# Moving four of a batch tile's gathers from layer 1 of the tile before it to layer 2 of the tile before that, with GpSimd's products moved the other way

## The reference

```python
e = jnp.stack([tbl_0[ids[:, 0]], ..., tbl_31[ids[:, 31]]], axis=1)       # (1024, 32, 16)
xk = x0 = e
for W in (W0, W1, W2):                                                   # (32, Hk-1, 64)
    xk = relu(einsum('bmd,bhd,mhk->bkd', x0, xk, W))
    outs.append(sum(xk, axis=2))
h = concatenate([concatenate(outs, axis=1), dense_ctx], axis=1)          # 192 + 16 columns
h = maximum(h @ W_top1 + b_top1, 0); h = maximum(h @ W_top2 + b_top2, 0)
y = h @ W_top3
```

## Time and profile before

| | us |
|---|---|
| median of three runs | 651.5 |
| the profiled execution | 648.11 |
| its span | 646.1 |
| PE, DVE, POOL, ACT busy in the span | 576.5, 558.0, 513.1, 349.6 |
| one round in the middle (322.9 to 393.8) | 70.9 |
| DVE, PE, POOL busy in that round | 70.38, 69.69, 61.67 |

### The profile page before, as it was taken

One profiled execution on the slowest core, in us unless ns is written; L12 is line 12 of the kernel. 1 busy time (PEld: TensorE's weight loads), 2 busy tenths in 40 slices (PEclk: granted clock), 3 DMA queues, 4 the chain that ended last, 5 costly groups with the idle time before them and its releaser, 6 DMA issues.

```text
span 646.1 us, 8375 instructions
## 1 busy us (share of the span) xinstructions
PE 576.5 (89%) x2992; PEld 194.5 (30%) x2992; DVE 558.0 (86%) x520; ACT 349.6 (54%) x537; POOL 513.1 (79%) x373
## 2 busy tenths in 40 slices
PE   0027799999999699999999999999999999999998
PEld 0002112322343133432243223432343324333444
DVE  1002899899998699999999999999999999999993
ACT  0002664455665357666666557555667657656751
POOL 6777769488888888888888888888898876477770
PEclk9999899999999899999999999999999999999999
DMA  8649998990189925996399918995499829890000
GB/s 258 175 46 249 244 203 203 245 228 4 11 173 228 240 63 98 230 214 167 33 224 196 237 26 165 224 189 130 71 252 204 182 27 219 166 280 5 1 2 0
DMA packets 89386, 98.70 MB, mean 153 GB/s; under 512 B 60833, under 2 KB 67362, under 8 KB 89330
## 3 DMA queue, kind: packets, MB, share of 16 engines
q1 hardware_dynamic: 77058, 90.12, 63.6%
q0 software_dynamic: 8192, 2.11, 3.3%
q10 hardware_dynamic: 4096, 5.95, 2.9%
HBM read 95.00 MB, written 7.61 MB: 159 GB/s over the span
## 4 chain that ended last, share of the span: by engine, by line
DVE 39%; PE 17%; issue 10%; ACT 6%; DMA 5%; SPq 0%; DVEq 0%
DVE z L760 37%; PE acc L529 15%; DMA x0rep<-x_rows 5%; ACT xk L615 4%; DVE row_sums L742 2%; ACT xk L590 1%; ACT xk L608 1%; PE top L446 1%; ACT xk_copy L626 0%; PE top L437 0%; PE top L434 0%; SPq L307 0%; PE acc L525 0%; PE acc L486 0%; DVEq L758 0%
## 5 line engine op out<-in xcount | busy, mean ns | idle before, releaser
L760 DVE TENSOR_TENSOR z<-xk,x0rep 128x1024 f32<-128x1024 f32 x463 | 530.3, 1228 | 42.2 <-DMA x0rep<-x_rows 27.5
L529 PE MATMUL acc<-z,w_sb 128*64 128x512 f32 x1852 | 443.8, 601 | 22.7 <-DVE z L760 20.4
L412 POOL TENSOR_TENSOR z_pool<-x0rep,xk_copy 128x1024 f32<-128x1024 f32 x113 | 268.3, 2377 | 48.3 <-PE acc L529 30.7
L366 POOL DMA_INDIRECT emb<-tbl,idx x256 | 244.7, 956 | 68.7 <-issue 61.7
L529 PEld LDWEIGHTS acc<-z,w_sb 128*64 128x64 f32 x1852 | 123.1, 137 | 309.3 <-issue 158.6
L615 ACT ACTIVATE xk<-xk_copy 32x1024 f32<-32x1024 f32 x128 | 130.5, 1019 | 111.4 <-DVE z L760 110.2
L529 PE MATMUL acc<-z_pool,w_sb 128*64 128x512 f32 x452 | 116.3, 593 | 0.4 <-POOL z_pool L412 0.4
L626 ACT ACTIVATE xk_copy<-acc 64x512 f32<-64x512 f32 x128 | 75.2, 587 | 2.2 <-PE acc L529 1.0
L608 ACT ACTIVATE xk<-lay 128x1024 f32<-128x1024 f32 x16 | 16.4, 1028 | 85.2 <-DVE z L760 48.3
L423 PE MATMUL acc<-w_sb 128*64 128x512 f32 x48 | 12.8, 678 | 44.0 <-DMA emb<-tbl,idx 44.0
L529 PEld LDWEIGHTS acc<-z_pool,w_sb 128*64 128x64 f32 x452 | 31.8, 137 | 62.5 <-issue 58.1
(11 more groups left out here) (40 smaller groups left out, 91.0 us busy)
## 6 DMA issues: line engine op xcount, KB each, us to landing
x0rep<-x_rows SPq DMA_DIRECT2D x128, 512.0 KB, 16.5
lay<-x_rows SPq DMA_DIRECT2D x32, 512.0 KB, 10.8
emb<-tbl,idx POOLq DMA_INDIRECT x256, 2.7
w_long<-w ACTq DMA_DIRECT2D x4, 768.0 KB, 6.8
squares<-x_rows SPq DMA_DIRECT2D x16, 128.0 KB, 2.2
x_rows<-emb SPq DMA_DIRECT2D x7, 256.0 KB, 4.6
x_rows<-emb SPq DMA_DIRECT2D x9, 128.0 KB, 6.1
w_sb<-w_long ACTq DMA_DIRECT2D x8, 128.0 KB
```

What stands on the lines that cost most here:

```text
L366: pool.indirect_dma_start(out=emb[:, i % 2, m, :], out_offset=None, in_=tables[m], in_offset=bass.IndirectOffsetOnAxis(ap=idx[:, i, m:m + ...
L412: pool.tensor_mul(z_pool[:, (count - 1) % POOL_RING, :], x0rep[:, g % X0_GROUPS, slot, :], xk_copy[:, side, :]).then_inc(z_pool_ready, 1)
L529: mm = pe.matmul(bank[c * H:(c + 1) * H, :], w[:, tile, :], src[:, c * COLS:(c + 1) * COLS], start=(k == 0), stop=last)
L760: dve.tensor_mul(z[:, (count - 1) % RING, :], xk[:, bank, :], src).then_inc(z_ready, 1)
```

## The change

The number of gathers in layer 2 goes from 16 to 20 of a tile's 32, and those in layer 1 from 16 to 12. POOL's share of products goes from 3 to 4 in 1A and 1B of tiles 1 to 6, and from 4 to 2 in 2B of tiles 1 to 5. In tile 0, 2B goes from 4 to 3. The shares of tile 7, and those of layer 2 in tile 6, stay at 5. In a full round POOL keeps 13 products and 32 gathers, and DVE 59 products. Over the kernel DVE makes 462 products where it made 463.

```diff
     if i == 0:
-        return {(1, A): 0, (1, Bs): 5, (2, A): 3, (2, Bs): 4}[layer, side]
+        return {(1, A): 0, (1, Bs): 5, (2, A): 3, (2, Bs): 3}[layer, side]
     if i == NT - 1 or (i == NT - 2 and layer == 2):
         return 5
-    return 4 if (layer, side) == (2, Bs) else 3
+    return {(1, A): 4, (1, Bs): 4, (2, A): 3, (2, Bs): 2}[layer, side]
...
-POOL_AT = {0: (), 3: (4, 8, 11), 4: (3, 6, 9, 11), 5: (2, 4, 6, 8, 10)}
+POOL_AT = {0: (), 2: (5, 10), 3: (4, 8, 11), 4: (3, 6, 9, 11), 5: (2, 4, 6, 8, 10)}
...
-EARLY = 16
+EARLY = 20
```

## The result

The changed kernel takes 646.31 us in the median of 11 runs (644.28 to 648.74). The kernel before took 650.75 us on the same chip in 11 runs (648.97 to 655.32). The ratio, taken over all runs and not from the two medians (which lie 4.4 us apart), is 0.9916, with a 95% interval of 0.9893 to 0.9938: 5.5 us faster, between 4.0 and 7.0. The forecast was 2.3 us faster, 649.2 us. The sign was right and the time lies in the range, 0.3 us from its lower end, but about half of the gain was not in the sum (2.1 of 4.4 us by the medians, 3.2 of 5.5 by the ratio).

What follows compares the result with a forecast made beforehand. It took DVE's 70.4 us round and a 70.9 us loop through A's load as bounds, PE at the end. Of PE's 4.1 us lead 2.3 would arrive: 651.5 - 2.3 = 649.2 us, range 646.0 to 653.0.

Steps and rivals of the forecast that it cites:

- the first step: Tile 2's last gather: four more gathers hide in POOL's idle time before 2B of tile 0; load and release 2.7 us sooner.
- A's path around the loop: Later rounds, release to release through POOL's 1B, last gather and A's load: 29.3 + 41.7 = 71.0 us.
- the loop as bound: Middle rounds of the kernel before: a path closing through A's load sets 70.92 us, above DVE's own 70.4.
- what is given back in tile 7: Tile 7's landing moves only 1.9 us sooner, so of PE's 4.1 us ahead 2.3 reach the end.
- the 0.4 us in hand: 1B of tile 7: DVE's product is ready 0.4 us before PE takes it, added to the gain reaching the end.
- The straight line: Release behind A's issue, interpolated on how far B follows A: 40.7 us at 15.2, 42.7 at 22.6; slope 0.27.
- the whole lead arrives: Rival: spare transfer time in tile 7 or rounds of 70.4 us let 4.1 us or more reach the end; 647.3 us, 22%.
- A longer loop: Rival: A's load takes 42.7 us whatever B does and gathers add 0.25; rounds of 72.25 us, 654.9 us in all, 11%.
- PE's clock: Rival: the granted clock falls in the longer 2B of the steady rounds, costing 5 us; 654.2 us, 3%.
- wait for `z_pool`: Sign of a wrong forecast: PE waits in 2B for POOL's products; they were expected about 60 us after release, wanted at 64.
- the DVE wait of 1 to 2.5 us: Sign of a right forecast: in 0B of tile 7 DVE waits for `x0rep`, or ACT's second fill, 1 to 2.5 us.
- faster by over 0.5%: Whole kernel: outcome class beyond measurement noise, from most of the 647.3 us rival and the forecast's top; 28%.

Runs made afterwards that it cites:

- before_front: Kernel before with all eight gathers of 1B dealt out ahead of POOL's first product of 1B; ratio 1.0019.
- before_again: Kernel before, unchanged, run again for a second trace; 692.27 us on the slow-starting kind of chip.
- before_third: Kernel before, unchanged, run for a third trace; 687.05 us on the slow-starting kind of chip.
- after_again: Changed kernel, unaltered, run again for a second trace; ratio 0.9964 to the kernel before on the chip of 690 us.
- after_third: Changed kernel, unaltered, run once more beside its two parts; ratio 0.995 to the kernel before on a chip of 688 to 690 us.
- y_late_before: Kernel before with the wait for y, the ctx transfer and y's write moved behind side B's load; ratio 0.9909.
- y_late_after: Changed kernel with the wait for y, the ctx transfer and y's write moved behind side B's load; 641.17 us, ratio 0.9838 to the kernel before.
- run 40: Not a follow-up run: part of the sentence that on some chips the first 100 us take 40 us longer.

## Why the prediction was right or wrong

**Right: the first step.** The load of tile 2 starts 2.78 us sooner (2.7 forecast). POOL's product at 126.71 still has 5.15 us idle before it, so the four gathers were hidden:

```profile
126.71 2.37 POOL L412 TENSOR_TENSOR z_pool<-x0rep,xk_copy 128x1024 f32<-128x1024 f32 x1 [5.15 <-issue]
...
171.14 0.98 POOL L366 DMA_INDIRECT emb<-tbl,idx  x1 [0.16 <-issue]
```

Of it 1.75 reached the release in this trace, not 2.7: A's load took 41.8 us against 40.7, with B following by the same 15.2. The mean of three traces each is 2.6.

**Right: A's path around the loop.** Tile 3's POOL in 1B, first product and the tile's last gather:

```profile
301.39 2.38 POOL L412 TENSOR_TENSOR z_pool<-x0rep,xk_copy 128x1024 f32<-128x1024 f32 x1 [0.52 <-issue]
...
312.27 0.98 POOL L366 DMA_INDIRECT emb<-tbl,idx  x1 [0.16 <-issue]
```

Release to first product 9.42 us (9.44 forecast), to the end of the gather 11.86 (11.85), to A's issue 8.28 (8.00), to the release of tile 4 41.76 (41.7): 71.3, with the only wait of the middle in it, 0.96 us. B is issued 48.8 us behind the release (49.5).

**Wrong in its reason, small in effect: the loop as bound.** The prediction read 9.44 + 10.79 + 8.00 + 42.69 = 70.92 as a loop that closes through A. Any start splits a round into terms that sum to it; that they do is no sign of a bound. before_front took 1.6 to 6.2 us out of the first three terms in tiles 4 to 7 and the fourth, 42.69, grew to 44.5, 47.7, 48.6 and 50.6. The bound was B: 50.87 + 20.05. With it, the change is good for the round: B's path is 2 us shorter (48.8 + 20.05 = 68.9), A's is longer by one product less one gather (29.6 + 41 = 70.6 with a load as in tiles 3, 5 and 6), and what is left is DVE's 70.3 in three rounds of four. I had 71.0 for all. The four rounds took 282.3 us where I had 283.4, and this 1.0 us made good the 0.95 that was missing at tile 2's release. That the table agrees at tile 6 (2.38 for 2.15) is luck in this pair of traces.

**The step that failed: what is given back in tile 7.** "The landing moves by 1.1 + 0.27 x 3.0 = 1.9 us." It moved by 3.28. Here B follows A by 23.0 us before, 20.1 after, and the release comes 41.2 and 39.2 behind A's issue, 18.2 and 19.1 behind B's. The slope on B's start is 2.1 in 3.0, 0.7, not 0.27: B's load was the bound in this tile of before too. The other traces have it as well: the release is 42.2 and 41.1 us behind A's issue in before_again and before_third, 39.4 and 39.8 in after_again and after_third. ACT's second fill of 0B in after:

```profile
569.68 1.03 ACT L608 ACTIVATE xk<-lay 128x1024 f32<-128x1024 f32 x1 [5.57 <-DMA lay<-x_rows]
```

It ends at 570.71, before at 573.79, 3.1 sooner. With 3.28 for 1.9, and the 0.4 us in hand as forecast, the sum gives 3.7 us, and the traces show 3.53. The straight line was drawn through 15.2 and 22.6 as if they lay on one slope; they lay on two sides of a bend. The prediction's rival "the whole lead arrives" (22%) comes near in its number, 4.2 us, but its reason, spare time in tile 7, does not hold: in before slot 2 of B landed at 574.49, 0.1 us ahead of the product that needs it, and in after DVE waits 1.22 us for it. The lead came through because the landing moved with B's issue.

**Not in the sum at all: what the timed runs have beyond the traces.** The step above is worth 1.4 us of the 3.2 that the sum lacks. The first two traces differ by 3.53 us behind the start and 3.2 in all, the timed runs by 5.5 (4.0 to 7.0). The profiled execution of before (648.11) is below all 11 timed ones beside it, though one run of the same kernel on the other chip of this kind took 646.37; that of after (644.91) lies among its own. Late landings like the one in tile 3 of before_again cost the kernel before whatever they last. B has 1.4 us of spare in after (70.3 - 68.9), so small ones should cost it less. That is argued, not shown: the changed kernel's three traces lie 4.5 us apart, those of before 5.4, and the dip behind y's write is in both kernels. Some 2 us of the gain stay open.

**Rivals.** A longer loop did not come: rounds stayed at 70.3 to 71.3. PE's clock stayed at 1.00 in the middle. PE did not wait for `z_pool`. Tile 7 shows the DVE wait of 1 to 2.5 us that was told, 1.22.

**The chance.** I gave "faster by over 0.5%" 28%. The arithmetic moved the median in step with the trace, 648.11, though the times on hand put the median 3.4 us above it. A trace that beats all timed runs was a reason to look for what the slower ones suffer from, and to widen on the fast side.

## What to carry to other kernels

A release that waits for two loads in one queue is the later of two sums, not a weighted mean: work out both paths, and find where the second load's issue falls after the first has drained. A chain of terms that adds up to the round proves nothing; what shows that a path is not the bound is that one of its terms grows when another is shortened. And look at what stands in the queue ahead of a large load: a few bytes per partition at that place can cost as much as a whole rearrangement gains.

## What the runs showed of the hardware that I had not expected

- A write of 128 pieces of 4 bytes, issued just ahead of a 5 MB load, is followed by some 4 us or more in which the rate falls from about 240 GB/s to 80 to 184, and to 32 where the queue had run dry, with the DMA engines 0.75 to 1.20 busy. Issued 8 us later it gave 5.5 us over six tiles, some 0.9 us each.
- On some chips the first 100 us run 40 us longer, with one matmul in 2.8 us and SP's 31 issues of line 280 spread over 36.0 us (before_again) in place of 19.2 (before), while the DMA share is 1.05 at 233 GB/s. The rest of the kernel runs as on the others.
- A's and B's loads, 10.5 MB at about 240 GB/s, bring slot 2 of B 39 to 42 us behind A's issue if B is issued within some 20 us of A. Where B's issue comes 22 us behind A's or later, the product that needs the slot starts 18.2 to 21.5 us behind B's issue in the traces of before and before_front (23.2 once). With y's write and the wait for y behind B's load, as in y_late_before and y_late_after, the slot lands 35.5 to 39.3 us behind A's issue.
